# A two-layer attention and feed-forward block in float32: the first feed-forward product on two groups of tokens at a time, and a new order of the work on all engines

## What is computed

```python
x = x + attention16(layernorm(x), ctx)          # A: 16 heads of 16, q, k, v with biases, w_o
t = layernorm(x)                                # B
h = relu(t @ w1 + b1)                           # 256 -> 1024 (only expert 0 has a weight)
x = x + (layernorm(t + h @ w2 + b2) * gamma + beta)      # Y
x = x + attention1(layernorm(x), layernorm(ctx))         # C: one head over 77 keys
t = layernorm(x)                                # D
idx = argmax(pe @ sign(sigs).T)                 # one of 8 tiles for each position, the same in both batches
x = x + t @ W[idx] + b[idx]
```

## Time and profile before

| | |
|---|---|
| device time, median of 3 runs | 274.83 us (274.8 to 275.03) |
| span of the profiled execution, first to last instruction | 272.0 us |
| time of the profiled execution itself | not listed apart from its span; 2.8 us lie between the span and the median |
| instructions in the span | 6214 |
| TensorE busy | 249.2 us (92%) |
| VectorE busy | 220.3 us (81%) |
| GpSimd busy | 189.7 us (70%) |
| ScalarE busy | 160.7 us (59%) |
| mean granted TensorE clock | 0.982 |

### The profile page before, as it was taken

How to read it: one execution, slowest core, us unless ns; L and a number is a source line. 1 busy time by engine, 2 the same in 40 slices (tenths; PEclk the granted TensorE clock), 3 DMA queues, 4 the chain that set the end, 5 groups by cost and what they waited for, 6 DMA issues and landing times.

```text
span 272.0 us, 6214 instructions
## 1 busy us (share of the span) xinstructions
PE 249.2 (92%) x2048; PEld 221.2 (81%) x2048; DVE 220.3 (81%) x573; ACT 160.7 (59%) x510; POOL 189.7 (70%) x361
## 2 busy tenths in 40 slices
PE   1969899899799999999999999999999997989990
PEld 1758676699798879998898799989899996867880
DVE  2899999999998889954999985898587589976551
ACT  3559795864363868695385896457645173465430
POOL 3367788987958896775497788878785497427354
PEclk9995999999999999999999999999999999999997
DMA  6992020011101182000002321121160000000032
GB/s 175 329 326 89 0 81 0 2 39 42 39 2 40 41 265 86 14 9 2 0 2 63 76 77 42 58 60 40 57 217 2 0 0 2 0 2 2 39 154 116
DMA packets 11156, 17.61 MB, mean 65 GB/s; under 512 B 1377, under 2 KB 7509, under 8 KB 11125
## 3 DMA queue, kind: packets, MB, share of 16 engines
q1 hardware_dynamic: 9333, 11.98, 13.9%
q0 software_dynamic: 1792, 5.24, 6.4%
HBM read 14.07 MB, written 3.15 MB: 63 GB/s over the span
## 4 chain that ended last, share of the span: by engine, by line
PE 68%; DVE 15%; POOL 5%; ACT 5%; issue 4%; DMA 1%; SPq 0%; POOLq 0%; DVEq 0%; ACTq 0%
PE PB L266 29%; PE PB L259 12%; PE PB L464 9%; PE S L387 5%; PE PB L339 5%; PE PB L399 4%; PE S L377 4%; ACT E L1066 2%; DVE SX L659 2%; POOL E L1263 1%; DMA WKV<-in_w_k 1%; DVE SX L673 1%; POOL SM L1220 1%; DVE HL L686 1%; DVE XTL L638 1%
## 5 line engine op out<-in xcount | busy, mean ns | idle before, releaser
L1263 POOL TENSOR_TENSOR E<-E,SX 128x308 f32<-128x308 f32 x64 | 43.8, 712 | 10.7 <-DVE SX L676 10.4
L1066 ACT ACTIVATE E<-S,SX 128x77 f32<-128x77 f32 x128 | 39.4, 336 | 10.6 <-DVE SX L659 10.6
L266 PE MATMUL PB<-XTH,W1H 128*128 128x256 f32 x128 | 37.7, 295 | 1.5 <-DVE XTL L638 1.4
L266 PE MATMUL PB<-W2H,HH 128*128 128x256 f32 x128 | 37.6, 294 | 0.0
L266 PE MATMUL PB<-XTL,W1H 128*128 128x256 f32 x128 | 36.2, 283 | 0.0
L266 PE MATMUL PB<-XTH,W1L 128*128 128x256 f32 x128 | 36.2, 282 | 0.0
L266 PE MATMUL PB<-W2H,HL 128*128 128x256 f32 x128 | 35.5, 278 | 0.0
L266 PE MATMUL PB<-W2L,HH 128*128 128x256 f32 x128 | 35.5, 278 | 0.0
L1220 POOL TENSOR_TENSOR SM<-SM,nhalf 128x2 f32<-128x2 f32 x40 | 28.3, 707 | 3.1
L1089 ACT ACTIVATE HH<-PB 128x512 fp32r<-128x512 f32 x32 | 19.0, 598 | 18.0 <-PE PB L266 18.0
L1076 ACT ACTIVATE EW<-S 124x640 f32<-124x640 f32 x32 | 21.9, 711 | 10.9 <-PE S L387 10.1
(11 more groups left out here) (203 smaller groups left out, 725.2 us busy)
## 6 DMA issues: line engine op xcount, KB each, us to landing
RAW<-in_w SPq DMA_DIRECT2D x4, 512.0 KB, 6.3
WD<-in_WD SPq DMA_DIRECT2D x8, 256.0 KB, 4.6
X<-in_x SPq DMA_DIRECT2D x4, 256.0 KB, 5.4
x<-X SPq DMA_DIRECT2D x4, 256.0 KB, 2.1
E<-in_WD SPq DMA_DIRECT2D x4, 256.0 KB
bc<-in_rows SPq DMA_DIRECT2D x1, 640.0 KB, 5.6
X<-in_w1r SPq DMA_DIRECT2D x1, 512.0 KB, 6.6
RT<-in_WD SPq DMA_DIRECT2D x2, 256.0 KB, 2.9
```

The costliest lines, as they stand in the source:

```text
L266: t = e.matmul(dst, a, b, start=first and j == 0, stop=last and j == n - 1)
L1066: t = e.activation(Ei[:, h * NK:(h + 1) * NK], P[:, at:at + NK], ACT.Exp, bias=SX[:, i, 0, k:k + 1], accum_out=SX[:, i, 1, k:k + 1])
L1263: t = e.tensor_tensor(Eh, Eh, SX[:, i, 2, 8 * a + h:8 * a + h + 4].unsqueeze(2).to_broadcast([128, 4, NK]), ALU.mult)
```

## The change

The first product takes a pair of groups: `w1(G, u)` makes one block of 128 hidden features for 512 tokens in six matmuls, after the low parts of both groups are there. `hh` and `hl` follow it, `w2` stays per group. `XBH`, `XBL` and twice as large `HH`, `HL` hold the pair; to make room, the 15 weight tiles lie in `OWN` (0), over `KBH` and `KBL` (1 to 4), in `E` (5 to 8) and in `EW` (9 to 14), and `XTE` lies over a part of `HH`. Stages B and Y get a third slot. On VectorE, dependent pairs are separate steps with other work between them in the list: `smax`/`ssub`, `ssum`/`srec`, `x2a`/`x2b`, `xr`/`x3_`, and the routing in single instructions. `cm` becomes two fused instructions with a negated score. GpSimd's `rs` has one instruction less for A, C and D. `load_starts` has no bounds checks. All four lists are in another order. Lines of the lists are cut here to the stretches that matter.

```diff
@@ load_starts
             values = nc.values_load_multi_w_load_instructions(EV[0:1, row, 0:NP], engines=[e.engine],
-                                                              min_val=0, max_val=most)[1]
+                                                              min_val=0, max_val=most, skip_runtime_bounds_check_because=
+                                                              "a count of 7 comparisons times a positive constant")[1]
@@ tensor
-            def w1(g, j, p):
+            def w1(G, u, p):
                 w.wait_ge(s["wlo"], 2)
-                w.wait_ge(s["loB"], g + 1)
-                P = hold(("w1", g, j), ("B", p), ("hl", 4 * g + j + 1))
-                for v in range(2):
-                    fs = slice((2 * j + v) * 128, (2 * j + v + 1) * 128)
-                    t = three(P[:, v * 256:(v + 1) * 256],
-                              [((W1H[:, c, fs], W1L[:, c, fs]), (XTH[:, 3, c, :], XTL[:, 3, c, :])) for c in range(2)])
-                t.then_inc(s["w1"], 1)
+                w.wait_ge(s["loB"], 2 * G + 2)
+                P = hold(("w1", G, u), ("B", p), ("hl", 8 * G + u + 1))
+                us = slice(u * 128, (u + 1) * 128)
+                three(P[:, :], [((W1H[:, c, us], W1L[:, c, us]), (XBH[:, c, :], XBL[:, c, :])) for c in range(2)]).then_inc(s["w1"], 1)
...
             def w2(g, i, h, p=None):
                 w.wait_ge(s["wlo"], 4)
-                w.wait_ge(s["hh"], 4 * g + 2 * h + 2)
-                w.wait_ge(s["hl"], 4 * g + 2 * h + 2)
+                w.wait_ge(s["hh"], 8 * (g // 2) + 4 * h + 4)
+                w.wait_ge(s["hl"], 8 * (g // 2) + 4 * h + 4)
...
+            pv(1, 1); sc(2, 1, 0, 1); f_m(2); wo(1, 1); sc(2, 1, 1, 0); tB(0, 0); r_perm(2); q(3, 1); tE(2, 0, 0, 1)
+            f_q(0); tB(1, 3); tE(2, 0, 1, 1); f_c(); w1(0, 0, 2); w1(0, 1, 3); sc(3, 0, 0, 1); sc(3, 0, 1, 0)
+            w1(0, 2, 1); w1(0, 3, 0); tE(2, 1, 0, 0); w1(0, 4, 2); w1(0, 5, 3); w1(0, 6, 1); tE(2, 1, 1, 1)
+            w1(0, 7, 2); w2(0, 0, 0, 0); sc(3, 1, 0, 1); sc(3, 1, 1, 0); tA(4, 1); w2(0, 0, 1); w2(0, 1, 0)
...
+            tE(7, 1, 0, 1); tC(4, 3); tE(7, 1, 1, 0); pv(7, 0, 2); pv(7, 1); cs(4, 3); wo(7, 0); tD(0, 2); cp(4, 1)
+            tB(6, 3); pr(0, 0, 0); tB(7, 2); co(4); tD(1, 3); w1(3, 0, 2); w1(3, 1, 0); w1(3, 2, 3); w1(3, 3, 2)
@@ vector
                 for i in range(2):
                     step(e.bn_stats(smi(K, g, i, 0, 6), src[:, i, :]))
-                settle()
-                for i in range(2):
+                for i in range(2):
+                    w.wait_ge(s["d"], steps[0] - 1 + i)
                     e.bn_aggr(smi(K, g, i, 6, 8), smi(K, g, i, 0, 6)).then_inc(s["var" + K], 1)
...
                 e.tensor_reduce(top, sv, AX, ALU.max, negate=True).then_inc(s["mx"], 1)
-                if apart(g, i, a):
-                    w.wait_ge(s["mx"], n + 1)
...
+            def ssub(g, i, a):
...
+                w.wait_ge(s["mx"], n + 1)
+                if g:
+                    w.wait_ge(s["tE"], n - 3)
...
+            def srec(g, i, a):
+                n, hs = 4 * g + 2 * i + a, slice(8 * a, 8 * a + 8)
+                made_here(("sums", n)) if apart(g, i, a) else w.wait_ge(s["ex"], n + 1)
...
-                e.tensor_tensor(P_, sv, CTB[:, g // 4, :].unsqueeze(1).to_broadcast([128, 2, NK]),
-                                ALU.add).then_inc(s["ca"], 1)
-                w.wait_ge(s["ca"], g + 1)
-                step(e.tensor_reduce(S_[:, 0, :], P_, AX, ALU.max))
-                settle()
-                e.tensor_scalar(S_[:, 1, :], S_[:, 0, :], -1.0, None, ALU.mult).then_inc(s["cm"], 1)
+                for i in range(2):
+                    e.tensor_tensor_reduce(PP[:, i, :], bank("cs", g)[:, i * NK:(i + 1) * NK], CTB[:, g // 4, :], 1.0, BIG,
+                                           ALU.add, ALU.min, accum_out=PS[:, g % 2, 1, i:i + 1]).then_inc(s["cm"], 1)
...
+            vb(1); smax(2, 0, 1); apply("B", 0); ssub(2, 0, 1); r_position(8); smax(2, 1, 0); f_m(); srec(2, 0, 0)
+            ssum(2, 0, 1); x1(1); srec(2, 0, 1); stats("B", 1); r_index(0); srec(2, 1, 0); r_index(1); lo("B", 0)
+            r_index(2); apply("B", 1); kbl(1); r_index(3); r_pairs(0); f_q(); lo("B", 1); smax(2, 1, 1); r_pairs(1)
+            ssub(2, 1, 1); ql(3); f_c(); hl(0, 0); hl(0, 1); smax(3, 0, 0); smax(3, 0, 1); ssub(3, 0, 1)
+            ssum(2, 1, 1); hl(0, 2); stats("A", 4); r_pairs(2); srec(2, 1, 1); r_pairs(3); hl(0, 3); hl(0, 4)
+            apply("A", 4); hl(0, 5); r_pairs(4); hl(0, 6); srec(3, 0, 0); hl(0, 7); smax(3, 1, 0); smax(3, 1, 1)
+            ssub(3, 1, 1); ssum(3, 0, 1); srec(3, 0, 1); r_pairs(5); stats("A", 5); y(0); srec(3, 1, 0)
@@ gpsimd
-                if K != "Y":
+                if K in "ACD":
+                    w.wait_ge(s["rs" + K], g + 1)
+                    e.tensor_scalar(smi(K, g, 1, 10, 11), smi(K, g, 1, 6, 7), smi(K, g, 1, 9, 10), -1.0,
+                                    ALU.mult, ALU.mult).then_inc(s["mr" + K], 1)
+                if K == "B":
                     e.tensor_tensor(sm(K, g, 11), sm(K, g, 6), minus[:, :], ALU.mult).then_inc(s["nm"], 1)
@@ sync
-            load_weights(range(8))
-            load_weights((14,))
+            load_weights((0,))
...
+            w.wait_ge(s["sc"], 32)
+            load_weights(range(1, 5))
             w.wait_ge(s["tE"], 32)
-            load_weights(range(8, 12))
-            w.wait_ge(s["wo"], 8)
-            load_weights((12, 13))
+            load_weights(range(5, 9))
+            w.wait_ge(s["pv"], 16)
+            load_weights(range(9, 15))
```

More of the change, by code:

```diff
@@ L19 @@
 EPS = 1e-5
+BIG = 3.0e38
 SIGNALS = (
@@ L912, in f_stats, with r_bias @@
+            def r_bias(k):
+                last()
+                if k == 0:
+                    rstep(e.tensor_tensor(eq[:, :, 0:7], in1(SID[:, :], 7), in0(V[:, 0, 1:8], 8), ALU.is_ge))
+                elif k == 1:
+                    rstep(e.tensor_reduce(mx[:, 0, :], eq[:, :, 0:7], AX, ALU.add))
+                else:
+                    e.tensor_copy(EI[:, :], mx[:, 0, :]).then_inc(s["ei"], 1)
             def f_stats():
```

579 lines of the change are left out of this document (313 added, 266 removed).

## The result

The changed kernel takes 286.56 us (median of 4 runs, 282.22 to 288.6) against 274.89 for the old one beside it: a ratio of 1.0317 [1.0273, 1.0362]. It is slower; the forecast was 267.6 and lies on the other side. The profiled execution took 285.43 us, with a span of 283.7, 11.7 above the old one's 272.0. The same changed kernel scatters by 2% from run to run, so for it a microsecond between two kernels means little. Kernels are therefore compared by their ratios: 1.0317 is 8.7 us, and a difference of 0.01 between two ratios is 2.75 us.

The account below looks back on a forecast made before the run. VectorE's work was taken to bound the first 72 us, TensorE's columns the next 145, latency the 33 after. Gains of 4.3 + 1.9 + 1.0 = 7.2 us took 274.8 to 267.6, own range 264 to 271.

Parts of the forecast that it names:

- TensorE's columns in the next 145: From 72.2 to 217 us TensorE, busy 144.77 of 144.80 us, was taken as the bound, so its columns count.
- Step 1: First product on TensorE: 192 matmuls of 512 columns replace 384 of 256; gain 2.5 us, ends 0 and 5.0.
- Step 2: VectorE's first 72 us: less work ahead of the second group's low part, then TensorE bound; 4.3 us gained, ends 0 and 8.5.
- the 3.7 of the pairs: VectorE's waits inside 31 dependent pairs ahead of the milestone, 0.12 us each, taken to vanish: 3.7 us.
- Step 3: Rest of VectorE's work, bounds checks and routing: hidden where TensorE never stops, costed at nothing; 5.38 us stall shrinks to 1 to 2.
- Step 4: Weight tile fetches: the last six land by some 205 us, well ahead of their use near 253; effect nothing.
- Step 5: The last group's tail: fused second-attention steps 0.35, a GpSimd step going twice 0.4, separate reciprocal 0.2; gain 1.0 us, ends 0.3 and 2.
- (a): Front bound by the chain over GpSimd, ScalarE and VectorE, not VectorE's list; only 2.5 + 1.0 gained, 271.3 us; chance 0.14.
- (b): Front bound by TensorE's own work: 8.5 us gained there, 261.6 us in all; chance 0.17.
- (d): 512-column matmul costs as much as two and the order merely shifts waits: 274.8 us, within 0.5; chance 0.04.
- (c): Pairing itself loses: TensorE's 5.7 us filler between a pair's groups goes, 11.5 us lost over four pairs, 279.1 us; chance 0.09.

Follow-up runs that it names:

- w1_high: Old kernel with the weights of the query, w_o and the first product declared behind the value matrix, at SBUF's far end: 274.91 us, ratio 0.9993.
- no_checks: Old kernel without the run-time bounds checks in the reads of run starts, nothing else: 274.83 us, ratio 0.999.
- re_before: Old kernel with only the order of all four lists (and PSUM banks) changed, to one worked out by search from trace durations: 296.33 us, ratio 1.0707.
- before_re: Old kernel with its own front kept up to 43 us and a searched order behind it: 278.44 us, ratio 1.0168.
- old_front_re: Changed kernel with the old kernel's front order, a searched order behind 46 us, and weights and hidden blocks at SBUF's far end: 278.81 us, ratio 1.0147.

## Why the prediction was wrong, step by step

**What bounds the kernel.** "TensorE's columns in the next 145" failed. TensorE was busy all the time, but w1_high took 2 to 3 us of work from it and the end did not move. By the table of lost time it lost 10.5 us between 72 and 208 us, in waits too short to be shown and in steps slower than their shortest. That what one engine saves it then waits for in the next place is my explanation; no run follows it step by step.

**Step 1** had its size right. Forecast 2.5 with a spacing of 0.2263; measured 0.2285 and 2.2. The rule of the Trainium skill, page "TensorE: Matmul & The Clock Gate", section "Wait — 56ns, not 53.3ns?", would have had 0.2158, and the row speaks against it for float32r. What was missing is the other product: I read one spacing, 0.1197, and counted it for both. The second product stood at 0.1135 and lost 1.7 to 2.3 when its operands moved. (The row of 60 that I read held 12 query and 48 first products, none of the second.) The declarations in the diff showed the move; I priced it at nothing by not pricing it.

**Step 2** is where the prediction failed, and in sign. The low part of the second group's tokens was to come at 57.1 and came at 69.17 (71.50 before):

```profile
69.17 0.69 DVE L673 TENSOR_TENSOR XBL<-PB,XBH 128x512 fp32r<-128x512 f32 x1 [0.35 <-ACT XBH L1117]
```

The sum took the steps that leave VectorE's list ahead of the milestone and subtracted them, as if a list's length set its time. The work did leave: up to the milestone VectorE is busy 62.92 us before and 52.82 after, 10.1 less, where the sum without the waits inside pairs had 10.7. (One small step and the two pivots even took 3.4 us more: 2.64 for 0.17, 1.71 and 1.77 for 1.27 each.) What failed is the other part of the milestone, VectorE's idle time. It was 8.6 us before, the sum had it fall by the 3.7 of the pairs, and it rose to 16.4. That is 11.5 of the missing 12.1 us. "With 14 us less to do VectorE will wait more" stood in the text, and I priced it at 1.0 with an end of 5. Of the idle time 6.6 us are five waits for score products of TensorE, which had none ahead of this milestone before; the longest comes behind TensorE's late start:

```profile
21.60 1.57 DVE L694 TENSOR_REDUCE SX<-S 128x8 f32<-128x616 f32 x2 [2.77 <-PE S L408]
```

The second half, TensorE from the milestone on, was then void: in lost time at 72 us, the gain of 4.3 became a loss of 9.6. The working also had an unexplained 83.5 where the row gives 83.06; that is 0.4 us and changes nothing here. Which of the moved steps make the waits stays open: each repair of a single place moved the wait, and only a new order of everything behind the front, with the old front, won 5 us.

**Step 3.** Right: no_checks shows no difference, and the stall is 0.70 in the new kernel, shorter than the 1 to 2 forecast.

**Step 4.** Nothing was seen of the weight tiles: the last six are issued from 207.4 us on, where they were to be there by some 205, and the last 64 products take 13.89 us before and after. It was not tried apart.

**Step 5.** The sign is right, the size too large. From the last y to the last products 0.4 was gained, not 1.0. The fused step is 0.23 us, 0.25 forecast, but each has a readout behind it (below). What each of the three parts brought was not tried apart.

```profile
245.71 0.23 DVE L765 CUSTOM_DVE_ANT_0 PP<-PB,CTB 128x77 f32<-128x77 f32 x1
245.87 0.08 DVE L765 DVE_READ_ACCUMULATOR2_ANT PS<- 128x1 f32 x1
```

**The rivals.** (a) came nearest: there are gaps of VectorE above 1 us before 57 us, but from 16 us on they are for TensorE (2.77, 1.09, 1.24), not for GpSimd, and the one for GpSimd, 1.13 us at 5.57, was 1.17 in the old kernel; and (a) had the time still faster. (b) and (d) fell. (c) had the sign and the wrong place: it asked for 1.8 us of idle time ahead of each paired product, and TensorE has none directly ahead of any; the nearest stops before the four, 1 to 6 us earlier, are 0.60, 0.46, 0.81 and 0.62. What it said in passing of the clock did come, elsewhere: at the first q and from 38.4 to 48.7 us. The slower side had 0.09 and one mechanism; that a new order of four lists can lose by itself, anywhere, was not among the cases at all, though the order was the largest part of the diff.

## What to carry to other kernels

Where several in-order lists are interleaved tightly, don't price a change of order by the work that leaves the busiest list: price the first stop it makes, follow who stands behind it, and give the side "slower" a real share whenever lists are rewritten. An engine that is shown as busy all the time can still lose time in waits too short to be shown, so less work on it need not mean less time; take a little of its work away in the old kernel (here by moving its operands) before building on it. To judge one part of a change that comes with a new order, give the old version an order of the same making, and more than one: re_before and before_re, two orders from one search for the old kernel, lie 15 us apart by their ratios.

## What was unexpected in the hardware

- Some orders scatter more than others: the new kernel's four runs lie 6.4 us apart, the four of old_front_re 0.9, on the same instructions but for their order and the places of some tiles.
